# Summing the gate logarithms of a gated linear attention by one fp16 product instead of two fp32 ones, with the chunk totals spread by a transfer

## What is computed

```python
g = jax.nn.sigmoid(x.reshape(B, L, H, d) @ gw.T)
g = jnp.clip(g, 1e-06, None)
log_c = jnp.clip(jnp.cumsum(jnp.log(g), axis=1), -30.0, 30.0)
Gc = (jnp.exp(log_c) + 1e-06)[..., None]
R = jax.nn.silu(K @ sw.T)[..., None]
S = jnp.cumsum(KV * R / Gc, axis=1) * Gc
out = jnp.einsum('blhd,blhde->blhe', Q, S).reshape(B, L, D)
```

## Time and profile before

| | us |
|---|---|
| time, median of 3 runs (lowest, highest) | 652.83 (652.31, 654.2) |
| the profiled execution: its time | 652.83 |
| its span from the first to the last instruction | 651.0 |
| busy: PE, PEld, DVE, ACT, POOL | 629.2, 546.5, 507.5, 435.3, 357.1 |

### The profile page before, as it was taken

How to read it: one execution, slowest core, us unless ns; L and a number is a source line. 1 busy time by engine, 2 the same in 40 slices (tenths; PEclk the granted TensorE clock), 3 DMA queues, 4 the chain that set the end, 5 groups by cost and what they waited for, 6 DMA issues and landing times.

```text
span 651.0 us, 21292 instructions
## 1 busy us (share of the span) xinstructions
PE 629.2 (97%) x7734; PEld 546.5 (84%) x7734; DVE 507.5 (78%) x1245; ACT 435.3 (67%) x999; POOL 357.1 (55%) x434
## 2 busy tenths in 40 slices
PE   3889999999999999999999999999999999999997
PEld 3668888888888888888888888888888888888886
DVE  5998888878787777877778877877787777878673
ACT  2688666767666776766677676667676666767662
POOL 4766465554555555456455555645555554655355
PEclk9999999999999999999999999999999999999999
DMA  9347755666746765554567856667656465677421
GB/s 309 94 124 121 111 140 135 148 142 131 111 117 129 138 132 139 135 119 112 130 139 136 143 130 97 132 136 129 143 130 135 106 125 128 141 128 127 100 45 34
DMA packets 186793, 83.05 MB, mean 128 GB/s; under 512 B 118320, under 2 KB 186160, under 8 KB 186688
## 3 DMA queue, kind: packets, MB, share of 16 engines
q1 hardware_dynamic: 184448, 79.05, 58.3%
q10 hardware_dynamic: 2240, 2.62, 1.2%
HBM read 12.43 MB, written 8.39 MB: 32 GB/s over the span
## 4 chain that ended last, share of the span: by engine, by line
PE 92%; DMA 3%; SPq 2%; DVE 1%; issue 1%; POOL 0%; POOLq 0%; DVEq 0%
PE y_bank L2251 17%; PE attn_bank L2195 9%; PE hid_b L2230 9%; PE hid_a L2230 9%; PE front_b L2132 7%; PE y_bank L2265 7%; PE front_a L2113 6%; PE front_b L2094 6%; PE score_a L2161 5%; PE attn_bank L2209 5%; PE score_b L2161 4%; PE attn_bank L2180 3%; PE hid_a L2232 2%; PE hid_b L2232 2%; DMA x_sb<-in_x 2%
## 5 line engine op out<-in xcount | busy, mean ns | idle before, releaser
L2251 PE MATMUL y_bank<-wproj_t,sq_h 128*128 128x256 f16 x512 | 118.5, 273 | 0.0
L2251 PE MATMUL y_bank<-wproj_t,sq_l 128*128 128x256 f16 x512 | 118.5, 273 | 0.0
L1727 DVE TENSOR_TENSOR sq_l<-relu_sq,sq_h 128x512 f16<-128x512 f32 x128 | 105.3, 824 | 1.0 <-ACT relu_sq L1032 0.9
L1680 DVE TENSOR_TENSOR masked<-score_a,shapes_sb 128x512 f32<-128x512 f32 x128 | 87.0, 680 | 16.0 <-PE score_a L2161 15.9
L1680 DVE TENSOR_TENSOR masked<-score_b,shapes_sb 128x512 f32<-128x512 f32 x128 | 87.2, 681 | 11.8 <-PE score_b L2161 11.7
L666 POOL TENSOR_TENSOR state_diag<-state,state_mask 128x256 f32<-128x256 f32 x56 | 53.4, 954 | 63.6 <-DVE state L1699 63.1
L1032 ACT ACTIVATE relu_sq<-relu_sq 128x512 f32<-128x512 f32 x128 | 79.6, 623 | 9.8 <-DVE sq_l L1727 9.7
L653 POOL COPY decay_halves<-decay 128x1024 uint16<-128x1024 uint16 x32 | 33.2, 1038 | 87.3 <-ACT decay L983 87.3
L697 POOL TENSOR_TENSOR y_both<-y_both,x_sb 128x512 f32<-128x512 f32 x32 | 41.2, 1287 | 70.0 <-DVE y_both L1739 70.0
L1023 ACT ACTIVATE sq_h<-relu_sq 128x512 f16<-128x512 f32 x128 | 79.2, 620 | 0.1
L933 ACT ACTIVATE vg<-front_b 128x304 f32<-128x304 f32 x64 | 27.2, 425 | 71.9 <-PE front_b L2132 71.8
(11 more groups left out here) (189 smaller groups left out, 1662.2 us busy)
## 6 DMA issues: line engine op xcount, KB each, us to landing
q_diag<-q SPq DMA_DIRECT2D x256, 64.0 KB, 2.7
k_stack<-k SPq DMA_DIRECT2D x128, 128.0 KB, 3.8
x_sb<-in_x SPq DMA_DIRECT2D x32, 256.0 KB, 3.3
out_y<-y_both SPq DMA_DIRECT2D x32, 256.0 KB, 3.4
relu_sq<-in_w_fc ACTq DMA_DIRECT2D x1, 1024.0 KB, 11.1
pj_nat<-in_w_proj ACTq DMA_DIRECT2D x1, 1024.0 KB, 13.8
y_both<-in_w_qk ACTq DMA_DIRECT2D x1, 512.0 KB, 4.6
w_stage<-in_w_qkvz_t SPq DMA_DIRECT2D x1, 512.0 KB, 6.3
```

Source lines behind the costliest of these rows:

```text
L1680: nc.vector.tensor_tensor(masked[:, c, g].rearrange("p (h n) -> p h n", h=4), score_bank[g % 2][:].rearrange("p (h n) -> p h n", h=4), cau ...
L1727: nc.vector.tensor_tensor(sq_l[:, q], sq[:, n], sq_h[:, q], ALU.subtract).then_inc(sq_l_done, 1)
L2251: last = mm(y_bank[:, c * D:(c + 1) * D], part[:, q, at:at + P], wproj_t[:, 2 * q + i], start=(q == i == c == n == 0), stop=False, skip_gr ...
```

## The change

- PE: `cumulate` becomes one fp16 product of 128x64: the triangle as fp16 (`causal16`) by both halves of the logarithms (`log16`, scaled by 1024), high and low parts in columns of their own.
- ACT: `log_high` (new) makes the high half; `decay_exp` scales by -1/1024. Once, `causal_taken`.
- DVE: `log_low` (new) makes the low half; `sums_taken` (new, a TENSOR_REDUCE over the bank) adds the two column groups into `chunk_sums`, after which the bank is free for `keys`; `clip_log` has an operation more, which adds `before`, and no longer reads the bank. `dens` uses SCALAR_TENSOR_TENSOR with a constant tile for both of its operations.
- SP: `spread_totals` (new) sends the last row of `chunk_sums` (the chunk totals, 32 numbers) to all 128 partitions.
- POOL: `sums_before` moves here from DVE, and adds the spread totals.
- The lists of all engines are written in another order; `unit_after(b, u, 4)` and `5` take the place of 3 and 4 in the steps of the normalisation, and `cumulate` stands in `slot` as `cumulate(*after)`, one period later than `cumulate(*unit_after(b, u, 3))`.

```diff
--- before
+++ after
@@ TensorE: keys and cumulate @@
-                    pe.wait_ge(log_c_done, upto(pb, pu, 1, 0))
+                    pe.wait_ge(sums_taken_done, upto(pb, pu, 1, 0))
...
-                pe.wait_ge(before_step, upto(b, u, 2, 0))
-                cum = front_a[:, 0:CH * H]
-                mm(cum, causal_sb, log_den[:].rearrange("p c h -> p (c h)"), start=True, stop=False)
-                mm(cum, ones[:], before[:, u % 2].rearrange("p c h -> p (c h)"), start=False,
+                pe.wait_ge(log_l_done, upto(b, u, 1, 0))
+                mm(front_a[:, 0:2 * CH * H], causal16[:], log16[:].rearrange("p s c h -> p (s c h)"), start=True,
                    stop=True).then_inc(cum_full, 1)
@@ ScalarE @@
+                nc.scalar.activation(log16[:, 0], log_den[:], ACT.Copy, scale=LOG_SCALE).then_inc(log_h_done, 1)
...
-                nc.scalar.activation(decay[:], log_c[:], ACT.Exp, scale=-1.0).then_inc(decay_done, 1)
+                nc.scalar.activation(decay[:], log_c[:], ACT.Exp, scale=-1.0 / LOG_SCALE).then_inc(decay_done, 1)
@@ VectorE: dens, log_low, sums_taken, clip_log @@
-                nc.vector.tensor_scalar(gate_den[:], exp_neg[:, :, 0:H], 1.0, 1e6, ALU.add,
-                                        ALU.min).then_inc(dens_done, 1)
-                nc.vector.tensor_scalar(write_den[:], exp_neg[:, :, H:2 * H], 1.0, None,
-                                        ALU.add).then_inc(dens_done, 1)
+                nc.vector.scalar_tensor_tensor(out=gate_den[:], in0=exp_neg[:, :, 0:H], scalar=1.0, in1=den_limit[:],
+                                               op0=ALU.add, op1=ALU.min).then_inc(dens_done, 1)
+                nc.vector.scalar_tensor_tensor(out=write_den[:], in0=exp_neg[:, :, H:2 * H], scalar=1.0,
+                                               in1=ones[:, 0:CH * H].rearrange("p (c h) -> p c h", c=CH),
+                                               op0=ALU.add, op1=ALU.mult).then_inc(dens_done, 1)
...
+                nc.vector.scalar_tensor_tensor(out=log16[:, 1], in0=log_den[:], scalar=LOG_SCALE, in1=log16[:, 0],
+                                               op0=ALU.mult, op1=ALU.subtract).then_inc(log_l_done, 1)
...
+                dve.wait_ge(cum_full, upto(b, u, 1, 0))
...
+                parts = front_a[:, 0:2 * CH * H].rearrange("p (s n) -> p n s", s=2)
+                nc.vector.tensor_reduce(chunk_sums[:, par].rearrange("p c h -> p (c h)"), parts, AX.X,
+                                        ALU.add).then_inc(sums_taken_done, 1)
...
                 dve.wait_ge(before_step, upto(b, u, 2, 0))
+                nc.vector.tensor_tensor(log_sum[:], chunk_sums[:, par], before[:, par], ALU.add).then_inc(log_sum_done, 1)
...
+                nc.vector.scalar_tensor_tensor(out=log_c[:], in0=log_sum[:], scalar=30.0 * LOG_SCALE, in1=log_limit[:],
+                                               op0=ALU.min, op1=ALU.max).then_inc(log_c_done, 1)
@@ SyncE: spread_totals @@
+                sp.wait_ge(sums_taken_done, upto(b, u, 1, 0))
...
+                last = chunk_sums[P - 1:P, par].rearrange("p c h -> p (c h)")
+                sp.dma_start(totals[:, par].rearrange("p c h -> p (c h)"),
+                             last.unsqueeze(1).to_broadcast([1, P, CH * H])).then_inc(totals_spread[par], 16)
@@ GpSimd: sums_before @@
+                pool.wait_ge(totals_spread[par], turned_upto(b, u))
...
+                nc.gpsimd.tensor_tensor(before[:, par, 1], before[:, par, 0], totals[:, par, 0],
+                                        ALU.add).then_inc(before_step, 1)
...
+                    nc.gpsimd.tensor_tensor(before[:, 1 - par, 0], before[:, par, 1], totals[:, par, 1],
+                                            ALU.add).then_inc(before_step, 1)
@@ the slot's list on TensorE, two lines @@
-                cumulate(*unit_after(b, u, 3))
+                cumulate(*after)
```

More of the change, by code:

```diff
@@ L1242, in prologue @@
+                values_gates(1, 0, 1)
+                gate_exp(1, 0)
                 rectified(0, 3, 0)
-                values_gates(1, 0, 0)
-                keys(1, 0)
-                values_gates(1, 0, 1)
+                z_high(1, 0)
+                squares_high(0, 2, 3)
                 rstd_guess(1, 2)
-                gate_exp(1, 0)
-                squares_high(0, 2, 3)
                 gate_log(1, 0)
+                squares(0, 2, 3)
+                log_high(1, 0)
+                squares_high(0, 3, 0)
@@ L2270, in slot @@
                 nxt, prev, after = unit_after(b, u, 1), unit_after(b, u, -1), unit_after(b, u, 2)
-                projected(b, u, 1)
                 queries_t(*unit_after(b, u, 3))
+                scores(*nxt, 1, 1)
+                state_update(*nxt, 0)
+                values(*nxt, 0)
+                scores(*nxt, 1, 2)
+                carried(*nxt, 0)
                 projected(b, u, 2)
+                scores(*nxt, 1, 3)
+                hidden(*nxt, 1)
+                hidden(*nxt, 2)
+                cumulate(*after)
                 state_update(*nxt, 1)
@@ L2276, in slot @@
                 carried(*nxt, 1)
-                hidden(*nxt, 2)
                 scores(*after, 0, 0)
@@ L2284, in slot @@
                 scores(*after, 0, 3)
[L2285 removed]
+                hidden(*nxt, 3)
+                values_gates(*unit_after(b, u, 3), 1)
+                hidden(*after, 0)
                 scores(*after, 1, 0)
[L2287 to L2298 removed]
+                projected(*nxt, 0)
+                projected(*nxt, 1)
             def prologue():
@@ L2395, in prologue @@
                 carried(0, 2, 0)
+                scores(0, 2, 1, 1)
+                scores(0, 2, 1, 2)
+                projected(0, 1, 2)
                 projected(0, 1, 3)
-                scores(0, 2, 1, 2)
                 scores(0, 2, 1, 3)
-                hidden(0, 2, 3)
-                keys(1, 0)
+                attn_projected(0, 1)
+                queries_t(1, 0)
                 state_update(0, 2, 1)
                 values(0, 2, 1)
+                carried(0, 2, 1)
                 scores(0, 3, 0, 0)
-                carried(0, 2, 1)
@@ L2422, in prologue @@
                 scores(0, 3, 1, 3)
-                carried(0, 3, 0)
-                projected(0, 2, 1)
                 keys(1, 1)
```

833 lines of the change are left out of this document (447 added, 386 removed).

## The result

The changed kernel takes 657.99 us (median of 4 runs, 657.36 to 658.86), the kernel before 652.88 beside it on the same chip: a ratio of 1.0076, 95% interval 1.0057 to 1.0095. It is slower, where 644.5 was forecast.

A forecast was written before the change was run, and what follows sets the result against it. TensorE, busy for the whole steady stretch, was taken to bound the kernel. From 652.83 us, less 8.8 for the product and plus 0.5 for the head, came 644.5; the range for 8 in 10 was 641 to 650.

The forecast's parts named there:

- Two of the prediction's stretches: TensorE's work between chain ends in a slot: 8.6 us ahead of cumulate, 4.8 us from cumulate to keys.
- The product's price: TensorE, each unit: fp32 cumulate's 0.37 us goes, one fp16 product of 0.095 comes; net 0.275, or 8.8 us over 32 units.
- Rival 1: TensorE: the short product is nearly free, 0.03 us, giving 642.4 us; chance 0.15.
- the waits that the change moves: Steady slot: chains into TensorE's new list all arrive with slack, from 1.1 to 3 us, so they cost nothing.
- slack 3: Behind cumulate: chain through the spread takes about 6 us; decay_exp on ACT needs it some 9 us after cumulate.
- slack 1.3 and 1.1: Slot's end: POOL's chain through split_decay reaches state_update 1.3 us and carried 1.1 us before TensorE needs them.
- DVE has 4 us of room a slot, and both forms are 0 on the path: DVE: dens in its new form costs nothing; gain 0 by the port rule, or 0.8 us of DVE a unit.
- Head: Before the steady part: reordered DVE steps and transfers cost +0.5 us, from -1.5 to +3; first scores near 40.3.
- The spread: Transfer of 32 numbers to 128 partitions: 0.6 us issue, landing taken as 3.8 us, covered by slack 3.
- Tail: End of the kernel: POOL's last attn_l may come a us earlier, but projected ends last; 0, at most -0.5 us.
- The slower one: Slot's end: split_decay makes POOL last at state_update and carried; 1.7 us late loses 16 us, 660; chance 0.07.
- Small stalls each slot: Steady slots: an engine held by the port pair, 0.15 us in each of 27 slots, 4 us: 648.5; chance 0.15.

The follow-up runs named there:

- runs 12: Kernel before's lists with one fp16 product; each partition adds its own sums, no totals spread, so part of the computation is left out: 647.63 us, ratio 0.9903.
- run 13: Kernel before's lists, nothing left out: two fp16 products of 64 columns, one with ones for the whole-chunk terms, no spread: 645.89 us, ratio 0.9879.
- run 16: Changed kernel with refine_rstd moved ahead of scale_y on VectorE, one line: 655.38 us, ratio 1.0033 to the kernel before.
- run 17: As run 16, and turn_decays one place earlier on SyncE, between turn_keys and store: 653.68 us, ratio 1.0005 to the kernel before.
- run 1: Changed kernel's lists on all engines with the kernel before's gate sums, no spread, dens in the old form: 660.4 us, ratio 1.0099 to the kernel before.
- run 2: Kernel before's lists with the new gate sums where the old stood; the decays' steps some 5 us later: 658.65 us, ratio 1.01.
- run 14: As run 2, but GpSimd adds each partition's own sums and no totals are spread, that part left out: 650.28 us, ratio 0.9947 to the kernel before.
- run 4: Changed kernel with the kernel before's order in one place of the head: rank_products behind group_sums, scale_columns(1) earlier: 657.39 us, ratio 1.0058 to the kernel before.
- run 15: Changed kernel, but GpSimd adds each partition's own sums and no totals are spread, that part left out: 656.01 us, ratio 1.0037 to the kernel before.
- run 3: Changed kernel with turn_decays first of SyncE's steps in a slot: 717.97 us, ratio 1.0991 to the kernel before.
- run 5: Changed kernel with clip_log earlier on VectorE, decay_exp earlier on ScalarE, turn_decays before turn_keys on SyncE: 667.92 us, ratio 1.02 to the kernel before.
- run 6: As run 4, and two token transpositions moved ahead of the q issues in SyncE's prologue: 658.68 us, ratio 1.0071 to the kernel before.

## Why the prediction was wrong

- **In us.** The profiled execution is 4.6 us longer than before where 8.3 less was forecast, a miss of 12.9. The 25 steady units were to take 477.3 - 25 x 0.275 = 470.5 and take 474.8, 4.3 of the miss. By the same reckoning some 6 us of it lie in the head, an estimate, and the rest behind the steady part. Two of the prediction's stretches are summed wrongly, 8.6 us for 8.7 ahead of `cumulate` and 4.8 for 4.5 ahead of `keys` (304.35 to 308.88), which changed no slack that decided.
- **The product's price: right mechanism, wrong size, to the good.** I took 0.095 us and a net of 0.275 a unit; the runs show 0.03 (runs 12 and 13), and 0.33 a unit. Rival 1, "nearly free", had the size, and my objection to it did not hold: what `state_update` costs the fp16 step ahead of it, 0.09, it cost `scores` in the kernel before. The Trainium skill, page "TensorE: Matmul & The Clock Gate", section "Back-to-back issue gap", has about 25 ns for a product this short; the 0.03 agrees with it, and I should have given it more than 0.15.
- **The step that failed is "the waits that the change moves".** I followed the chain behind `cumulate` to `decay_exp` (slack 3), and the POOL chain at the slot's end to `state_update` and `carried` (slack 1.3 and 1.1). Both held: `state_update` waited for `v_pad` 0.4 us in all. But `split_decay` has a second reader, and I did not follow it: `turn_decays`, which now stands behind `load`, `turn_keys` and `store` at the next slot's start, its landing of 3.1 to 6.1 us, `decay_transposed`, `chunk_out`, and the bank that `state_update(nxt, 1)` needs. This chain had no term in the sum, and in the slots where the landing took 4.7 us or more it had little slack or none: these slots hold 5.1 of the 5.9 us of stalls in the steady part, and two lines moved on the chain take 4.6 of them away (runs 16 and 17).
- **"DVE has 4 us of room a slot, and both forms are 0 on the path."** For `dens` this held: in run 1 the old TENSOR_SCALAR form of `write_den` takes 664 ns on average in the new list, the new form 657 in the changed kernel. In the old lists the new form is the slower one, 591 on average in run 2 against 319 before, which cost the steady part nothing (run 14). The error was to apply the port rule to the changed line alone. The new list put `refine_rstd` beside `residual`, 1.1 us longer as a median, and on the ring. Average room on an engine says nothing about a chain that crosses it. The page "SBUF — State Buffer", section "SBUF: two separate sides", of the Trainium skill has operations with two SBUF inputs blocked for the whole of a GpSimd instruction; newton's 1.26 us beside the 1.28 of `residual` agrees, and 0.16 where it stands alone.
- **Head: the second step that failed. +0.5 was taken, with +3 at most; it is 5.1 at the fourth unit,** though the first units' cheaper products are in it. The first `scores`, forecast within 1.5 us of 40.3, came at 41.78, just there, so that far the count held. The later 3.6 us are behind it, in a stretch that the prediction did not walk, where TensorE's idle time grew from 0.4 to 6.2 us, and run 4 shows that the early part is not worth its price: time won there was gone 40 us later.
- **The spread: priced well (3.1 us for 3.8), and its place too.** In these lists it is covered but for 2.0 us (run 15). In other lists it was worth 6.9 us (runs 2 and 14), so this is a property of the list and no law.
- **Tail: 0** held, with idle time of 4.7 us both before and after. What lies behind the steady part is still 2.0 us longer, as more of TensorE's work was left for it; no term had that.
- **The rivals.** The slower one gave 660 for a slot late by 0.6 us, near the number, but by the POOL chain, which never decided. "Small stalls each slot" had the sign of the cause, an engine held by the port pair, and 4 us of stalls. What no case had was both a head and a ring.

What was shown: the ring (runs 16 and 17), the spread's price in each list (2 and 14, the changed kernel and 15), the product's gain (12 and 13). What stays open is the head, at least as much of the miss as the ring: by single executions the late place of the decays costs 3.5 us there in the old lists, and the new lists cost 3.2 with the old sums. VectorE is busy 1.9 us longer there (110.30 against 108.37), but that this is on the path isn't shown, and no run gives the head back. Open too is why the turned decays land in 5.4 us in the late slots, in 4.1 as a median and in 3.2 in the kernel before.

## What to carry to other kernels

When the engine that bounds a kernel gets faster by 0.3 us a period, some ring through the others, invisible before, may be the new period, in all slots or only in those where a transfer lands late: follow every reader of every moved result once round, until it comes back to the bound engine, and sum that ring against the new period and not the old. On a queue that works in order, moving a transfer ahead is paid by what stands behind it: of the four moves ahead on SyncE here, against the changed kernel, one lost 9% (run 3), one 1.5% (run 5, with moves on two other engines), one gained nothing (run 6), and only the one by a single place gained, 1.7 us (run 17 against 16); moving a 2-element operation away from a GpSimd instruction gave 2.6 us. And a replacement that needs no new hand-over (run 13: one more 0.03 us product) can beat a smaller one that needs a transfer.

## What was not expected of the hardware

- Two fp16 products of 64 columns with different weights together take 0.06 us between an fp32 and an fp16 step (290.19 to 290.25); the two fp32 ones of 32 columns took 0.37.
- The fp16 step ahead of the fp32 `state_update` takes 0.09 us more, whether its last product has 256 columns (0.31 for a step of 0.22) or 64 (0.12 for 0.03). Ahead of `carried`, fp32 too, it does not: `hidden` takes 1.09 there and 1.09 ahead of an fp16 step (368.64 to 369.73).
- VectorE's operation on 128x2 numbers takes 0.16 or 1.26 us, and moving it by one line, away from the start of GpSimd's 1.28 us addition, gave the 0.16 (run 16).
- The spread of 32 numbers to 128 partitions lands in 3.1 us as a median, but in 5.22 in the slot of run 2 shown above, where `stack_keys` is issued right behind it; that this is why is only argued.
- With ScalarE and not SyncE issuing the spread, the old lists gain 3.5 us and the new ones nothing: the same edit, priced by the list around it.
- The transfer of the turned decays lands in 3.0 to 5.4 us in the kernel before and 3.1 to 6.1 in the changed one, and its long landings cost nothing until the ring was tight.
